# Cross-attention scores from split queries and keys, and two batches' latents normed at the first change

## What is computed

```
x = x + cross(ctx, layernorm(x), mask, ...)
def cross(c, latents, mask, ...):
    xn     = layer_norm(c, g1, b1)
    ln_lat = layer_norm(latents, g2, b2)
    q      = ln_lat @ Wq
    k, v   = split(concat([xn, ln_lat], axis=1) @ Wkv)
    weight = softmax(where(full_mask, (q / 8) @ k.T, -max), axis=-1)   # 16 heads of 64
    return (weight @ v) @ Wout
```

## Time and profile before

| what | us |
|---|---|
| three runs | 2174.29, 2176.55, 2178.16; median 2176.55 |
| span of the profiled execution | 2174.1 |
| start and first latent step | 0 to 63.57 |
| 12 chunk steps and 3 changes | 63.57 to about 680 |
| linear stage and six layers | about 680 to the end |
| one chunk step | 37.4 |

### The profile page before, as it was taken

The page is one execution under the profiler, slowest core; times in us unless marked ns, Lnnn a source line. Parts: engine busy times, 40 slices in busy tenths (PEclk is TensorE's granted clock), DMA queues, the critical chain, the costliest instruction groups (busy, mean ns, idle before and its releaser), DMA issues.

```text
span 2174.1 us, 49300 instructions
## 1 busy us (share of the span) xinstructions
PE 2095.3 (96%) x16360; PEld 1703.7 (78%) x16360; DVE 1677.4 (77%) x4800; ACT 1340.4 (62%) x3916; POOL 507.9 (23%) x290
## 2 busy tenths in 40 slices
PE   5999999999998998999999999999999999999988
PEld 4777877777786676888888888888888888888877
DVE  6776677677666497898889888888889888988872
ACT  2666566556655255676667666766676666766652
POOL 2111111111111332232223222232223222322210
PEclk9999999999999998999999999999999999999999
DMA  3000000000000400021112011201120111001000
GB/s 119 7 11 1 6 12 1 6 12 1 6 26 1 155 11 13 13 71 33 33 33 70 14 32 52 71 14 33 52 72 14 33 52 64 17 28 52 14 13 20
DMA packets 46990, 69.95 MB, mean 32 GB/s; under 512 B 9093, under 2 KB 33717, under 8 KB 46517
## 3 DMA queue, kind: packets, MB, share of 16 engines
q1 hardware_dynamic: 44405, 62.21, 9.4%
q10 hardware_dynamic: 2368, 4.98, 0.6%
HBM read 50.54 MB, written 1.05 MB: 24 GB/s over the span
## 4 chain that ended last, share of the span: by engine, by line
PE 53%; DVE 4%; issue 3%; DMA 3%; ACT 2%; POOL 1%; SPq 0%; DVEq 0%; ACTq 0%; POOLq 0%
PE ps_loc L1560 17%; PE ps_loc L1666 9%; PE ps_loc L1637 6%; PE ps_loc L1610 4%; PE ps_loc L1676 4%; PE ps_loc L1626 4%; PE ps_loc L1599 4%; DMA late<-y_all 3%; PE ps_loc L1579 3%; POOL rnorm L2467 1%; PE ps_loc L1220 1%; DVE norm L2089 1%; DVE w_low L2081 1%; ACT prob_loc L1889 1%; ACT work L1873 0%
## 5 line engine op out<-in xcount | busy, mean ns | idle before, releaser
L2467 POOL TENSOR_TENSOR rnorm<-norm_floor,half_loc 128x32 f32<-128x32 f32 x48 | 300.4, 6258 | 586.8 <-DVE norm_floor L2092 463.2
L1560 PE MATMUL ps_loc<-w_high,xT 128*128 128x512 f32 x1152 | 380.1, 411 | 0.7 <-ACT qk L1868 0.6
L1889 ACT ACTIVATE prob_loc<-prob_loc,top_loc 128x128 f32<-128x128 f32 x768 | 298.4, 398 | 46.7 <-DVE top_loc L2156 44.4
L1666 PE MATMUL ps_loc<-xnT_loc,w 128*128 128x256 f32 (+1 forms) x1056 | 255.1, 388 | 2.6 <-DVE kT_loc L2224 1.5
L675 ACT ACTIVATE prob<-prob,new_top 128x256 f32<-128x256 f32 x512 | 252.2, 497 | 0.0
L1560 PEld LDWEIGHTS ps_loc<-w_high,xT 128*128 128x128 f32 x1152 | 204.0, 189 | 50.7 <-issue 9.3
L2156 DVE CUSTOM_DVE_ANT_0 prob_loc<-ps_loc,const,rnorm 128x128 f32<-128x128 f32 x768 | 218.9, 347 | 27.9 <-PE ps_loc L1599 26.2
L857 DVE CUSTOM_DVE_ANT_0 prob<-ps_cross,bias 128x256 f32<-128x256 f32 x512 | 185.0, 421 | 65.6 <-PE ps_cross L456 51.0
L1881 ACT ACTIVATE qT_loc<-ps_loc 128x512 f32<-128x512 f32 x96 | 57.3, 597 | 285.5 <-PE ps_loc L1579 285.5
L1560 PE MATMUL ps_loc<-w_low,xT 128*128 128x512 f32 x576 | 227.6, 395 | 0.0
L1666 PEld LDWEIGHTS ps_loc<-xnT_loc,w 128*128 128x128 f32 (+1 forms) x1056 | 192.7, 191 | 29.6 <-DVE kT_loc L2224 2.6
(11 more groups left out here) (201 smaller groups left out, 4299.0 us busy)
## 6 DMA issues: line engine op xcount, KB each, us to landing
w_raw<-in_ffn_Wqkv_dram SPq DMA_DIRECT2D x24, 512.0 KB, 5.4
w_raw<-in_ffn_Wqkv_dram SPq DMA_DIRECT2D x24, 256.0 KB, 4.0
wo<-in_ffn_Wo_dram SPq DMA_DIRECT2D x24, 256.0 KB, 3.7
v_mid<-v_even SPq DMA_DIRECT2D x24, 256.0 KB, 3.4
v_mid<-v_odd SPq DMA_DIRECT2D x24, 256.0 KB, 3.5
w<-in_ffn_W_dram SPq DMA_DIRECT2D x12, 341.0 KB, 4.6
w<-in_ffn_W_dram SPq DMA_DIRECT2D x6, 640.0 KB, 4.9
ctx_raw<-in_ctx_dram SPq DMA_DIRECT2D x12, 256.0 KB, 2.7
```

Source lines behind the costliest of these rows:

```text
L1560: ins = pe.matmul(ps[:, DENSE + j % 2, :], xT[:, px, kk, t * P:(t + 1) * P], wqkv[pw][:, kk, col:col + 512], start=kk == 0 and n == 0, sto ...
L1666: ins = pe.matmul(ps[0:n, DENSE + m % 2, part * T:(part + 1) * T], w1[:, kk, col:col + n], xnT[:, kk, :], start=kk == 0, stop=kk == KD - 1)
L1889: ins = act.activation(pr, pr, ACT.Exp, bias=top[:, h, t:t + 1], scale=-1.0, accum_out=total[:, h, t:t + 1])
L2467: pool.tensor_tensor(rnorm[:, b % 2, t, :], norm2_floor[:, :], half[:, :], ALU.pow).then_inc(rnorm_done, 8)
```

## The change

1. Scores: `qT` gets a high and a low part, `kT` becomes the high part, and `kT_low` (two tiles in the room of the raw key weights) the low one, all f32r. Each f32 score matmul becomes three f32r ones, ordered so that the two row halves alternate.
2. ScalarE writes the high part of all four key groups and of the queries; VectorE writes the low parts as PSUM minus high (`keys_low`, `queries_low`). The banks come free with `k_done` and `q_done`, which VectorE now signals. `k01_done` is gone. In a step VectorE does the low parts of groups 0 and 1, then the next chunk's norm, then groups 2 and 3.
3. Norms: the start norms only batch 2's tiles, with the query low parts in between; those of batches 3 and 4 (four tiles) are normed in the first change, in `rest_of_latents`, behind the low parts of key groups 0 and 1.
4. Room: `o_norm` shares with `probT`, `inT` with the low part of its split. The linear stage's key and value weights are two tiles, loaded by 8 DMAs in place of 4.

The turnings stay where they were. The core of the diff:

```diff
             def scores(u, pair, banks=PAIR_SCORE):
+                if pair % 2 == 0:
+                    pe.wait_ge(k_done, u + 4 * (pair // 2 + 1))
                 if pair == 0:
-                    pe.wait_ge(k01_done, u + U)
                     pe.wait_ge(v_done, u)
                 if pair == 1:
                     pe.wait_ge(k_done, u + U)
                 pe.wait_ge(s_read, u + (2 * (pair - 1) if pair >= 2 else 0))
                 for t in range(TT):
-                    for i in range(2):
-                        head = slice(i * DH, (i + 1) * DH)
-                        ins = pe.matmul(ps[:, banks[pair % 2] + i, t * CHUNK:(t + 1) * CHUNK],
-                                        qT[head, pair, t * P:(t + 1) * P], kT[head, pair, :], start=True, stop=True)
+                    for n, (q_part, k_part) in enumerate(PARTS):
+                        keys_of = kT_part(k_part, slice(pair, pair + 1))
+                        for i in range(2):
+                            head = slice(i * DH, (i + 1) * DH)
+                            ins = pe.matmul(ps[:, banks[pair % 2] + i, t * CHUNK:(t + 1) * CHUNK],
+                                            qT[head, q_part, pair, t * P:(t + 1) * P],
+                                            keys_of[head].rearrange("p o n -> p (o n)"),
+                                            start=n == 0, stop=n == len(PARTS) - 1)
...
@@ ScalarE @@
             def attend(u, last, turn, uc=None):
+                keys_out(u, 0)
+                keys_out(u, 1)
                 probs_out(last, 0)
                 keys_out(u, 2)
...
@@ VectorE @@
+            def queries_low(turn, js=range(4)):
+
+                for j in js:
+                    dve.wait_ge(q_high, turn * 4 + j + 1)
+                    pairs = slice(2 * j, 2 * j + 2)
+                    dve.scalar_tensor_tensor(out=qT[:, LOW, pairs, :],
+                                             in0=ps[:, PROJ + j % 2, :].rearrange("p (g n) -> p g n", g=2),
+                                             scalar=-float(DH) ** -0.5, in1=qT[:, HIGH, pairs, :],
+                                             op0=ALU.mult, op1=ALU.subtract).then_inc(q_done, 1)
 
-            def keys_out(u):
+            def keys_low(u, js):
+
                 dve.wait_ge(s_full, u)
-                for j in (0, 1):
-                    dve.wait_ge(k_full, u + 4 * (j + 1))
-                    dve.tensor_copy(kT[:, 2 * j:2 * j + 2, :], ps[:, PROJ + j % 2, :].rearrange("p (i n) -> p i n", i=2))\
-                        .then_inc(k01_done, U // 2)
+                for j in js:
+                    dve.wait_ge(k_high, u + 4 * (j + 1))
+                    pairs = slice(2 * j, 2 * j + 2)
+                    dve.tensor_tensor(kT_part(LOW, pairs), ps[:, PROJ + j % 2, :].rearrange("p (i n) -> p i n", i=2),
+                                      kT[:, pairs, :], ALU.subtract).then_inc(k_done, U // 4)
...
@@ the start @@
             find_chunks()
+            queries_low(1, (0,))
             dve.wait_ge(x_in, 16)
-            latents(2, range(TT, B * TT))
+            second = range(TT, 2 * TT)
+            *_, last = norm(chain, lambda t: k.x[:, t, :], lats, 2, second)
+            chain.link(last)
+            queries_low(1, (1, 2))
+            *_, last = norm(chain, lambda t: lats[:, t, :], lats, 3, second)
+            last.then_inc(lats_done, 1)
+            queries_low(1, (3,))
+            keys_low(U, range(4))
...
@@ a chunk step @@
-                    keys_out(u)
+                    keys_low(u, (0, 1))
...
                     prepare_next((bits >> c) > 1)
+                    keys_low(u, (2, 3))
...
@@ change(turn) @@
-                keys_out(u)
+                queries_low(turn + 1)
+                keys_low(u, (0, 1))
+                if turn == 1:
+                    rest_of_latents()
                 prepare_next(bits > 0)
+                keys_low(u, (2, 3))
```

More of the change, by code:

```diff
@@ L152, in place_linear_weights @@
         self.lin_place = ExitStack()
-        self.wkv_in = self.sb("wkv_in", [P, KD, 2 * INNER], ctx=self.lin_place, side="right")
-        self.lin_wq = self.wkv_in[:, 0, 0:KD * D].rearrange("p (k n) -> p k n", k=KD)
-        self.lin_wkv = self.wkv_in[:, 1, 0:KD * 4 * D].rearrange("p (k s n c) -> p k s n c", k=KD, s=2, n=2)
+        with ExitStack() as shared:
+            self.wkv_in = self.sb("wkv_in", [P, KD, 2 * INNER], ctx=shared, side="right")
+        self.lin_wkv, self.kT_low = [None] * KD, [None] * KD
+        for kk in reversed(range(KD)):
+            self.lin_wkv[kk] = self.sb(f"lin_wkv{kk}", [P, 2, 2, D], ctx=self.lin_place, side="right")
+            self.kT_low[kk] = self.sb(f"kT_low{kk}", [P, PAIRS // KD, CHUNK], F32R, self.lin_place, "right")
+        self.lin_wq = self.sb("lin_wq", [P, KD, D], ctx=self.lin_place, side="right")
         self.lin_wq_in, self.lin_wkv_in = self.sem("lin_wq_in"), self.sem("lin_wkv_in")
@@ L248, in cross_attention @@
             dense_f = first("dense_f", [1, B])
+        with ExitStack() as shared:
+            o_norm = k.sb("o_norm", [P, TT, INNER], F32, shared)
         probT = sb("probT", [P, RING, KT, 512])
@@ L260, in cross_attention @@
         xn = sb("xn", [P, KT, D])
-        inT = sb("inT", [P, KD, CHUNK])
+        with ExitStack() as shared:
+            k.sb("inT_high_place", [P, KD, CHUNK], F32, shared)
+            inT = k.sb("inT", [P, KD, CHUNK], F32, shared)
         inT_parts = sb("inT_parts", [P, 2, KD, CHUNK], F32R)
@@ L287, in cross_attention, with kT_part @@
         PROJ, SCORE, TURN, OUT = 0, 2, 4, 6
+        def kT_part(part, pairs):
+            if part == HIGH:
+                return kT[:, pairs, :]
+            half, own = divmod(pairs.start, PAIRS // KD)
+            return k.kT_low[half][:, own:own + pairs.stop - pairs.start, :]
         PAIR_SCORE, FIRST_SCORE = (SCORE, PROJ), (SCORE, OUT)
@@ L726, in _ @@
             queries_out(U, 1)
-            keys_out(U, 2)
-            keys_out(U, 3)
+            for j in range(4):
+                keys_out(U, j)
             for part in range(2):
@@ L989, in batch, with rest_of_latents @@
                 chunks(dve, bits, step)
+            def rest_of_latents():
+                ln, rest = dve.snap(ln_reg), range(2 * TT, B * TT)
+                ch = Chain(dve, dve_step, dve.snap(step_reg))
+                hold(dve, dve_held)
+                *_, ready = norm(ch, lambda t: k.x[:, t, :], lats, ln, rest)
+                ch.link(ready)
+                *_, ready = norm(ch, lambda t: lats[:, t, :], lats, dve.snap(ln + 1), rest)
+                ready.then_inc(lats_done, 1)
+                dve.reg_add(ln_reg, ln_reg, 2)
+                done(ch)
             def change(turn):
@@ L1089, in _ @@
             for n in range(2):
-                root(2 + n, (B - 1) * TT)
+                root(2 + n, TT)
             pool.wait_ge(lats_done, 2)
@@ L1116, in change @@
                 hold(pool, pool_held)
+                if turn == 1:
+                    for n in range(2):
+                        root(pool.snap(ln_reg), (B - 2) * TT)
+                        pool.reg_add(ln_reg, ln_reg, 1)
                 ch = Chain(pool, pool_step, pool.snap(step_reg))
@@ L1429, in local_layers @@
         xnT = sb("xnT_loc", [P, KD, T])
+        k.lin_place.close()
         gate = sb("gate", [P, 2, T])
-        k.lin_place.close()
         qT = k.sb("qT_loc", [P, PAIRS, T], F32, ctx, "right")
```

36 lines of the change are left out of this document (18 added, 18 removed).

## The result

| | median of runs, us | profiled span |
|---|---|---|
| before | 2175.42 (2171.46 to 2178.16, 4 runs) | 2174.1 |
| after | 2183.45 (2181.25 to 2185.27, 4 runs) | 2179.4 |

The ratio is 1.0035, interval 1.0021 to 1.0049: slower by 8.0 us. The forecast was 8.4. Whether its terms were right as well is the matter of what follows.

The account below looks back on a forecast made before the run. TensorE, in its own order, was taken to bound the step. Terms -6 + 4.5 + 10.8 - 1 = +8.3 us on a 2174.1 span gave 2182.4, plus 2.45 for runs, say 2185; range 2181 to 2195 with 0.62.

Parts of the forecast that it names:

- Pace of the scores, 0.118 from the keys' row: Score matmuls: each start of a pair of row halves takes 0.118 us, as the f32r key matmuls do.
- Chunk step -0.5: Cross attention: each chunk step gets 0.5 us shorter, 12 of them 6, after a wait eats 0.6 of the saving.
- the walk to the turning behind pair 3: Chunk step traced on TensorE: pair 3 starts at 317.65 against 317.42, the next turning at 318.55 against 318.48.
- The key chain of groups 0 and 1: ScalarE's copy, then VectorE's subtraction: some 1.6 us against 2.4 of other TensorE work, so it costs nothing.
- Queries +1.5 a change: Three changes: late query banks cost 2.0 us together, less the body's 0.5; 3 x 1.5 = +4.5 us.
- Norms +10.8: First change: put-off norms take 9.3 us ahead of pair 1's scores, a lower clock 1.5 more; +10.8 us (9.3 to 12).
- Start -1: Start: 6.9 us less norm work on VectorE against 4.2 more for subtractions and late query banks; -1 us (+0.2 to -2.7).
- All the rest of the start follows them at VectorE's pace: Start: everything after the first minima, said to start at 40.2 to 41.2 us, keeps VectorE's pace behind them.
- The scores pace at 0.107: Rival: score starts take 0.107 us and the start gives all 2.7; time 2176, chance 0.20.
- The halves' weight loads queue: Rival: the second half's weight load waits for the first, 1.42 us a pair; time 2267, chance 0.07.
- Slower by more: Rival: loads overlap, but starts take 0.13 to 0.14 or a second stop comes at the change; 2195 to 2205, chance 0.06.
- The estimate of 2252: Score weight loads in series at 107 ns each, 12 a pair, 1.28 us a pair; a time of 2252.

Follow-up runs that it names:

- samehalf: Changed kernel with both heads' score matmuls put on row half 0; one run, 2263.07 us.
- shortcols: Changed kernel with the second and third product of every score covering 128 of the 256 keys; one run, 2181.52 us.
- turn23: Changed kernel with the turnings of pairs 2 and 3 moved ahead of the scores of pairs 1 and 3; 2175.73 us, ratio 1.0 to the kernel before.
- lateword: Changed kernel with VectorE making the queries' low part before loading the next batch's word at the change of batch; 2179.14 us.
- nodefer: Changed kernel with the norms of batches 3 and 4 back at the start; 2177.56 us, ratio 1.001 to the kernel before.
- starts: Changed kernel with TensorE's word loaded before its wait for the layer's columns and VectorE's between the first key low parts, at the start; 2181.7 us.
- gaps23: Changed kernel with the changes of gaps, turn23 and starts together; 2164.6 us, ratio 0.995 to the kernel before.
- allfour: Changed kernel with the changes of gaps23 and lateword together; 2158.96 us, ratio 0.9926 to the kernel before.
- four corners: Comparison of before, deferonly, nodefer and after: whole or split scores, norms at the start or put off; second chunk's keys at 101.05, 94.69, 108.71, 102.31 us.
- deferonly: Kernel before with only the norm of the last two batches' latents put off to the first change, scores whole; 2176.83 us, ratio 1.0005.
- onehalf: Changed kernel with each query tile's three score matmuls of head 0 ordered ahead of head 1's three; one run, 2182.57 us.
- gaps: Changed kernel with the put-off norm cut in pieces between query low parts and at the step's end; 2170.09 us, ratio 0.9978 to the kernel before.

## Why the prediction was right, step by step

- **Pace of the scores, 0.118 from the keys' row: right**, to the last digit (0.355 us for three). The reason given, same type and widths, holds: one half alone goes at 0.118 a matmul as well (samehalf), and the two halves load side by side (shortcols).
- **Chunk step -0.5: the step is -0.73.** The mechanism held; the term that was mis-sized is the walk to the turning behind pair 3. It had that turning 0.07 us later than before (318.55 against 318.48), and it starts 0.10 earlier (12.72 us into the step, 328.90 from 316.18, against 12.82). Pair 1 itself came when the walk had it (9.07 us into the step, 9.09 said; the wait is 0.64 and not 0.8 because pair 0 ran longer). But VectorE's minima started 8.93 us into the step, not 9.09 (325.11, above), so pair 3 did not have to wait and stood at 11.82, not 11.99: Pairs 4 to 7 then gave 0.63 instead of 0.5. "0.6 of saving is eaten by the wait" was right in kind: turn23 gives 0.46 back. The key chain of groups 0 and 1, put at "nothing", was right but for the first chunk step, where it cost a wait of 0.99 us: there ScalarE comes late from the latent step's exponentials.
- **Queries +1.5 a change: right.** 1.63 us of wait against 1.7; a change with its step costs 0.8 and 1.0 more, where 2.0 - 0.5 - 0.5 = 1.0 was the sum. Its reason, the word's load in VectorE's queue, is shown by lateword for 1.3 to 1.4 us of it.
- **Norms +10.8: right.** The passes took 9.6 us (9.3 said). The stop of 9.64 stands in place of one of 0.6, 9.0 more, and the slower clock behind it makes up the rest to 10.7 (after against nodefer), 1.7 where 1.5 was said.
- **Start -1: wrong in sign,** +1.3 by the second chunk's keys, 2.8 us from the two terms' -1.5; of the other four profiles with that start none has these keys earlier than before either (101.38 to 102.67 against 101.05, the one profile of before). The first minima came at 40.15, at the early end of the 40.2 to 41.2 that were said. The step that failed is "All the rest of the start follows them at VectorE's pace": the rest took 0.9 to 1.6 us more in the profiles of that start, with TensorE at a lower clock. The load of TensorE's word behind a wait had not been looked for in the order of the program either; moving both engines' loads gave 0.6 to 2.3 us by the second chunk's keys (starts, gaps23, allfour). By the four corners the split's side is 7.6 us, where 6.9 less 1 leaves 5.9 for it in the sum, and the deferral's 6.4, not 6.9.
- **The rivals.** "The scores pace at 0.107" was out: 0.118, and the start gave nothing, so its 2176 had no leg. "The halves' weight loads queue" was out by the chunk step; samehalf shows that its price was right. "Slower by more" was not needed. The estimate of 2252 beside the queued loads comes out at about 2251 when its terms are added again.
- **The sum** came out close because errors of opposite sign met: seven plain steps 1.2 us better, the last piece 1.6 and change 1 0.5 better, the start 2.8 worse. The closeness of the total is luck to that extent; the main terms were right one by one. The last piece is 74.07 us in deferonly, with the code of before, against 75.74, so most of its 2.1 may be spread between profiles and no effect.

## What to carry to other kernels

Where a change gives a saving in the body and defers work to one place, ask first whether that place can be cut up: the norms cost 10.7 us in one block ahead of a key part and 2.4 in the same engine's idle times. Look behind each new wait for work that could stand ahead of it, and compare its length with the wait's: a turning of 1.02 us in a wait of 0.64 made the step slower, two turnings in two waits made it faster. A start in which engines hand work to one another is no place for differences of large estimates; there the two parts should be priced apart, each walked to the end, with the clock.

## What the runs showed of the hardware

- With three score matmuls of one row half ahead of three of the other in the program, the matmuls of both halves started in pairs (onehalf), and the step was the same (36.70 and 36.66 us). On one half alone they went one by one, 0.118 us each (samehalf).
- For f32r with 128 weight columns and 256 streamed, a start took 0.118 us, and 0.113 with a third of the streamed columns left out (shortcols).
- Behind the stop of 7.18 us in deferonly the granted clock was 0.50 (1.2 GHz) over 231.68 to 235.40, as it was below full behind the 6.62 us at the start of before and behind the 4.84 us at the start of after (0.52 over 39 to 46 us). Without the stop the clock stayed at 2.4 GHz over the whole step (gaps).
